# Four-layer sandwich kernel on one core: gathers, sums, first loads, rank products and late statistics take other places in the order written out by hand

## The reference

```
x = x + LN(ssm(LN(x)))       # A: selective state space scan with a short convolution
x = x + LN(moe(LN(x)))       # B: 8 experts, top 2
x = x + LN(attn(LN(x)))      # C: gated attention in groups of 32, with a linear part
x = x + LN(ffn(LN(x)))       # D: silu(x Wg) * (x Wu), then Wd
# moe: out += ((a * sigmoid(b)) @ Wo.T + bo) * comb[e],  a, b = split(x @ W1[e].T + b1[e])
```

## Time and profile before

| | us |
|---|---|
| median of 3 runs | 582.27 (581.85 to 584.56) |
| profiled execution, its own time | 578.57 |
| its span | 576.8 |
| PE busy, DVE busy | 484.9, 455.9 |
| POOL busy, ACT busy | 310.9, 306.6 |

### The profile page before, as it was taken

The page is one execution under the profiler, slowest core; times in us unless marked ns, Lnnn a source line. Parts: engine busy times, 40 slices in busy tenths (PEclk is TensorE's granted clock), DMA queues, the critical chain, the costliest instruction groups (busy, mean ns, idle before and its releaser), DMA issues.

```text
span 576.8 us, 11015 instructions
## 1 busy us (share of the span) xinstructions
PE 484.9 (84%) x3102; PEld 396.1 (69%) x3102; DVE 455.9 (79%) x1742; ACT 306.6 (53%) x655; POOL 310.9 (54%) x349
## 2 busy tenths in 40 slices
PE   7998998899898987678678687888888998889990
PEld 3555787697786866456555465777888897778890
DVE  3885678999898899967574467888888988799974
ACT  3767775667657562244243344565555566445531
POOL 5852553726677667657432657377787232224342
PEclk9999998999999999999798798999999999999996
DMA  7704999900000001335356764321212000000111
GB/s 192 233 2 119 286 285 285 276 6 9 20 25 15 27 11 36 91 105 173 123 166 183 218 197 147 118 56 56 73 50 63 1 2 0 2 1 20 37 38 55
DMA packets 74213, 54.87 MB, mean 95 GB/s; under 512 B 5665, under 2 KB 69665, under 8 KB 74154
## 3 DMA queue, kind: packets, MB, share of 16 engines
q1 hardware_dynamic: 69034, 41.58, 24.6%
q0 software_dynamic: 5120, 12.59, 7.5%
HBM read 19.70 MB, written 34.45 MB: 94 GB/s over the span
## 4 chain that ended last, share of the span: by engine, by line
PE 39%; issue 21%; DVE 18%; POOL 12%; ACT 5%; DMA 1%; SPq 1%; another core or an unknown queue 1%; POOLq 0%; DVEq 0%; ACTq 0%
PE ps L1907 5%; POOL z_rows L557 5%; PE ps L1909 4%; PE ps L1908 4%; POOL tails L705 2%; PE ps L2303 2%; PE ps L2369 2%; POOL work L680 2%; DVE rstats_t L1248 2%; PE ps L2228 2%; PE ps L2371 2%; DVE X L1210 1%; PE ps L2128 1%; PE ps L2394 1%; PE ps L1924 1%
## 5 line engine op out<-in xcount | busy, mean ns | idle before, releaser
L570 POOL DMA_INDIRECT shared_buf<-g_rows,back x64 | 64.1, 1001 | 37.5 <-DVE slot_g L1693 21.4
L557 POOL DMA_INDIRECT z_rows<-Z,dest x64 | 64.3, 1004 | 24.5 <-issue 16.6
L1907 PE MATMUL ps<-w_hi,ZT_hi 128*128 (+1 forms) x110 | 47.8, 435 | 18.3 <-issue 11.9
L823 ACT ACTIVATE Z<-X,shift,rstds 128x128 f32<-128x128 f32 x128 | 53.3, 484 | 11.8 <-DVE shift L1174 8.6
L1009 ACT ACTIVATE half_tanh<-ps 128x256 f32<-128x256 f32 x78 | 29.2, 384 | 53.7 <-PE ps L1909 40.7
L542 POOL TENSOR_TENSOR rstds<-vars_t,mhalf 128x4 f32<-128x4 f32 (+1 forms) x24 | 31.4, 1308 | 47.5 <-DVE vars_t L1197 24.8
L1693 DVE SCALAR_TENSOR_TENSOR slot_g<-half_tanh,ps 128x256 f32<-128x256 f32 x78 | 31.5, 416 | 29.8 <-ACT half_tanh L1009 17.5
L547 POOL TENSOR_TENSOR res_rstd<-rvar,mhalf 128x4 f32<-128x4 f32 x24 | 25.2, 1051 | 38.8 <-DVE rvar L1265 38.8
L1908 PE MATMUL ps<-w_lo,ZT_hi 128*128 (+1 forms) x110 | 41.7, 379 | 0.0
L1909 PE MATMUL ps<-w_hi,ZT_lo 128*128 (+1 forms) x110 | 41.4, 377 | 0.0
L1907 PEld LDWEIGHTS ps<-w_hi,ZT_hi 128*128 128x128 f32 x110 | 21.9, 199 | 27.5 <-issue 26.4
(11 more groups left out here) (359 smaller groups left out, 1568.3 us busy)
## 6 DMA issues: line engine op xcount, KB each, us to landing
z_rows<-zero SPq DMA_DIRECT2D x34, 512.0 KB, 6.6
g_rows<-slot_g SPq DMA_DIRECT2D x38, 256.0 KB
slot_zs<-z_rows SPq DMA_DIRECT2D x78, 64.0 KB
X<-in_x SPq DMA_DIRECT2D x4, 512.0 KB, 6.5
RES<-in_W1T SPq DMA_DIRECT2D x4, 512.0 KB, 5.6
out<-X SPq DMA_DIRECT2D x7, 256.0 KB, 2.3
z_rows<-Z,dest POOLq DMA_INDIRECT x64
shared_buf<-g_rows,back POOLq DMA_INDIRECT x64
```

Source lines behind the costliest of these rows:

```text
L557: pool.indirect_dma_start(z_rows[group(i)], bass.IndirectOffsetOnAxis(ap=dest[:, i, k, c:c + 1], axis=0), Zr[i % 4][:, c], None).then_inc( ...
L570: pool.indirect_dma_start(got[:, c, k], None, g_rows[group(i)], bass.IndirectOffsetOnAxis(ap=back[:, i, k, c:c + 1], axis=0))\
L823: act.activation(dst[:, c], X[:, i, c], ACT.Identity, bias=bias[:, c:c + 1], scale=rstd[:, c:c + 1]).then_inc(z_made, 1)
L1907: pe.matmul(dst, lh, rh, start=start, stop=False)
```

## The change

`gather(t)` waits for tile 2t + 4 of group 1 instead of 2t + 1. The sums and what hangs on them come two tiles later (`MOE_AT`, statistics). Of the fourteen calls of `SCATTER_TILE` the last eleven wait one or two tiles longer. The loads of group 1's first quad stand behind the store of tile 35, those of the next three behind the store of tile 38. On PE the rank computation stands behind the tile's product, and its five identity products are left out in the tile stage. Two powers and, at the end, `lastD(6)` move. The diff, with unchanged lines left out:

```diff
-        SCATTER_TILE = ((4, 2, 0), (4, 3, 2), (5, 0, 5), (5, 1, 7), (5, 2, 9), (5, 3, 11), (6, 0, 13), (6, 1, 15),
-                        (6, 2, 17), (6, 3, 19), (7, 0, 21), (7, 1, 23), (7, 2, 25), (7, 3, 27))
-        LATE_LOADS = {33: 0, 35: 1, 37: 2, 38: 3}
+        SCATTER_TILE = ((4, 2, 0), (4, 3, 2), (5, 0, 5), (5, 1, 9), (5, 2, 11), (5, 3, 13), (6, 0, 15), (6, 1, 17),
+                        (6, 2, 19), (6, 3, 20), (7, 0, 22), (7, 1, 24), (7, 2, 26), (7, 3, 28))
+        LATE_LOADS = {35: (0,), 38: (1, 2, 3)}
...
-        MOE_AT = (8, 10, 12, 14, 16, 18, 20, 22, 24, 26, 28, 30)
+        MOE_AT = (10, 12, 14, 16, 18, 20, 22, 24, 26, 28, 30, 32)
...
                     if g == 0 and j in LATE_LOADS:
-                        load_quad(QUADS.index((1, LATE_LOADS[j])))
+                        for late in LATE_LOADS[j]:
+                            load_quad(QUADS.index((1, late)))
...
-                if (i, c) == (5, 1):
+                if (i, c) == (5, 0):
                     power(1, SEQS - 1)
             for t in range(4 * CH):
-                pool.wait_ge(g_made, GTILES[0] + 2 * t + 2)
+                if t == 12:
+                    power(2, 0)
+                pool.wait_ge(g_made, GTILES[0] + 2 * t + 5)
                 gather(t)
                 if t == 9:
                     res_power(2, 0)
-                if t == 12:
-                    power(2, 0)
...
-                    if g == 1 and j == 30:
+                    if g == 1 and j == 32:
                         z(2, 0)
...
-                    if g == 1 and j in (20, 28):
-                        rbn_stats(2, (j - 20) // 8)
-                    if g == 1 and j in (21, 29):
-                        rbn_aggr(2, (j - 21) // 8)
-                    if g == 1 and j in (24, 33):
-                        x_add(2, (j - 24) // 9)
-                    if g == 1 and j == 25:
+                    if g == 1 and j in (22, 30):
+                        rbn_stats(2, (j - 22) // 8)
+                    if g == 1 and j in (23, 31):
+                        rbn_aggr(2, (j - 23) // 8)
+                    if g == 1 and j in (26, 35):
+                        x_add(2, (j - 26) // 9)
+                    if g == 1 and j == 27:
                         bn_stats(2, 0)
-                    if g == 1 and j == 26:
+                    if g == 1 and j == 28:
                         bn_aggr(2, 0)
-                    if g == 1 and j == 29:
+                    if g == 1 and j == 31:
                         scales(2, 0)
...
-                if half == 0:
-                    lastD(SEQS - 2)
             rbn_aggr(4, i)
+            lastD(SEQS - 2)
...
-                        for k in range(5):
-                            pe.matmul(bank(2)[:, 3 * P:4 * P], ident[:], ident[:], start=True, stop=True)
+                        if step < NT:
+                            for k in range(5):
+                                pe.matmul(bank(2)[:, 3 * P:4 * P], ident[:], ident[:], start=True, stop=True)
...
-                        elif j > 2:
-                            gate(NT + j // 2 - 1, 2)
                     slot_h(GFIRST[g] + j, n, j, experts[j - 4 * q])
+                    if g == 0 and 2 < j and j % 2 == 1 and NT + j // 2 - 1 < GATE_END:
+                        gate(NT + j // 2 - 1, 2)
```

## The result

In six executions of each, the kernel before had a median of 583.17 us (578.9 to 588.24) and the changed kernel 587.12 us (584.44 to 589.28). The ratio is 1.0098, with a 95% interval of 1.0067 to 1.0129: slower by about 1%. The changed kernel was timed twice more among the experiments, at 1.0058 [1.0022, 1.0093] and 1.0177 [1.0105, 1.0249]. The forecast of 579.1 was wrong, and 587.12 lies 1.1 above its range. The nearest of its cases is rival 2, the hole ahead of quad 1, at 585.6. That it comes so near is partly luck: its sum holds +4.3 us for a hole that measured +2.5.

The account below looks back on a forecast made before the run. Waits, not full engines, were taken to bound the tiles. Terms −1.5 + 0.8 + 2.8 − 3.0 − 1.0 − 1.25 = −3.15 us, carried to the median shown of 582.27, gave 579.1 us, range 573.5 to 586.0.

Parts of the forecast that it names:

- rival 2: Group 1's start: quad 1's loads wait for tile 38's gate, PE idles, clock falls again; +3.4 us, 585.6; chance 0.20.
- Late signals go by half: Tiles 8 to 11 of group 1: later gathers remove half of two 3.2 us ACT waits for PE; −3.0 us.
- the powers: POOL in group 1: its 2.66 us wait behind gather 9 for DVE's statistics nearly goes; −1.0 us.
- Rival 1: Group 1's gathers: POOL soon issues without a pause again, late signals stay; +0.35 us, 582.6; chance 0.24.
- Quads 1 to 3 behind the last store: Start of group 1: quad 1's loads wait for tile 38's gate and land after PE needs them; +2.8 us.
- Rank part with the scatters: Group 0: products ahead of ranks, no identity products, gain 2.8 us, limited by later scatters; −1.5 us together.
- the scatters bound the group from behind: End of group 0: six calls left instead of five, scatters end at 298.0, first loads start at 299 to 302.
- Quad 0 behind the store of tile 35: Between the groups: group 1's first loads wait for tile 35's gate and start 1.3 us later; taken as +0.8 us.
- Tail: Kernel's end: last statistics and power start earlier, one full DVE wait for POOL's addition stays; −1.25 us.

Follow-up runs that it names:

- c_best: Kernel before with the rank, gather and tail parts, without late loads and scatters: 573.60 us, 0.9890; again 577.96 us, 0.9949.
- a_loads: Changed kernel with group 1's first loads back behind the stores of tiles 33, 35, 37 and 38: 579.76 us, 0.9977 to the kernel before.
- c_nogather: Kernel before with the rank and tail parts alone, on the faster chip: 556.76 us, 0.9985.
- c_power: c_best with only the power of sequence 7 moved ahead of call (5, 1), on the faster chip: 559.45 us, 1.0035 to the kernel before.

## Why the prediction was wrong, step by step

1. *Late signals go by half (−3.0), and the powers (−1.0)*: this step failed, and it is the largest part of the miss that a run prices. The part alone measured −0.14%, 0.8 us, with zero in its interval, which ends at 0.9953; −4.0 us would be 0.993. Undone in the changed kernel, nothing came back. The trace shows why. I counted on the gaps between pairs of gathers. But the first gather moved with the first tiles from 311.73 to 320.44, tiles then ran ahead of POOL at about 1 us each, and ten gathers still stood nearly in one row. One late signal of 3.87 us stood at its end, where there had been two of 3.2. The wait of POOL for the statistics, counted as gone, is still 2.44 of 2.66 us. Rival 1, by which POOL soon issues without a pause again, was right in its mechanism.

2. *Quads 1 to 3 behind the last store (+2.8)*: right in mechanism, and in size for the hole. The hole from gate to gate is 2.5 us longer in the profile after, and 2.2 to 4.2 longer in the eight other profiles with quad 1 late. The point from which rival 2 was to decide, a PE idle time over 3 us and the lower clock behind it, was not met in the first profile: the idle time is 1.38 us, since the products ahead of it ran at the lower clock already and used up the rest. In the second profile of the changed kernel it was met (3.11 us, and 0.63 us for a product behind it), in the third it was 2.42. But filling the hole so that the clock held brought nothing back.

3. *Rank part with the scatters (−1.5)*: one sum for two things of opposite sign. The ranks alone give −0.40%, 2.3 us, but nothing in the changed kernel, where the transpose at tile 21 came 0.35 us earlier and not 2.1: I left out that the picks can come late by themselves. The scatter tiles cost: +0.3% alone (unclear), 0.9% between c_best and a_loads, about 0.8% on the faster chip. I had the last one end at 298.0, from two instructions more in the last burst; it ended at 301.25, since the pause before ended 1.9 us later and another tile was waited for. The step that failed is "the scatters bound the group from behind". On the slower chips no profile has a scatter in the chain ahead of the first load. What stands there in its place is a scatter row without pauses in group 0 and a late signal at its end; that this is how the scatters cost is argued from the profiles and not shown by a run of its own. The end of POOL's queue counts only on the faster chip (in three of its four profiles), and there I should have looked at all of its waits: POOL has 24 such instructions to its end, and a call that waits earlier moves all behind it.

4. *Quad 0 behind the store of tile 35 (+0.8)*: the first transpose came 2.95 us later. But gates up to tile 35 were late by 2.87 already, so this edit's own part is small, and putting quad 0 back brought nothing. Part of those 2.87 us can't be laid on the change: tile 5 was 2.0 us late (257.05 to 259.01), and so it was in the kernel with later gathers alone (259.24), which is the same up to there.

5. *Tail (−1.25)*: right, 1.45 us. The operation on four columns takes 1.25 us beside POOL's addition of 1.26 and ends with it; an operation of the same size takes 0.15 just ahead of it. The wait only moved to another of DVE's instructions. The Trainium skill states this in "SBUF — State Buffer", "SBUF: two separate sides": of a VectorE operation with two SBUF inputs and a GpSimd operation, the one that starts first has the shared ports for its whole length. The trace agrees: POOL's started at 573.95, DVE's at 573.97.

With 0.8 instead of 4.0 in step 1, my sum gives 582.3, within 0.5% of before. The other 4.8 us to 587.12 are the scatters, what the loads cost beyond their term, and the ranks' gain that is not there. The three measurements of the whole lie between +0.6 and +1.8%, so no division in microseconds holds for all of them. But it is known where the surplus sits: ranks, gathers and tail together measured 0.9890 and 0.9949, about their sum of 0.992, and the two costly parts cost more in company than alone (scatters 0.9 against 0.3%, loads 0.8 to 1.0 against 0.5%). Why they do is open; that parts cost more where PE waits less otherwise is argued, not shown. Also open is why the changed kernel has a lower clock between 223 and 290, ahead of the moved loads: 0.77, 0.85 and 0.87 in its three profiles, against 0.95 before. With the ranks and identity products back it was 0.92; but the ranks alone had 0.85 there and were faster, and the gathers alone, with the identity products, had 0.87.

## What to carry to other kernels

A wait that is put in front of a load is paid nearly in full when the consumer is only a few tiles behind (2.5 of 2.8 us here); read the distance from the load's issue to its use, and move only what is needed late (here quads 2 and 3 at most, and not quad 1). Delaying the start of a queue of long instructions doesn't thin it out if its producers run faster than the queue: count how many are ready when it starts. And price a table of waits over the whole queue, each entry by the wait that it can add, and edits of opposite sign in separate terms, so that an experiment can answer each. What a part is worth alone need not be what it is worth in company: the ranks' 0.4% was gone in the changed kernel.

## What was not expected of the hardware

- The chips differ. The kernel before took 581.2 to 583.2 us in five groups of runs and 557.5 in one, 4.3% less. On that chip the long waits of ACT for PE in the tile stage are nearly all gone, as the group of tanh of the whole page shows (busy, mean ns, idle before and its first releaser), for the ranks alone on a slower chip and then for c_nogather, which is the same kernel but for the tail (the kernel before has no profile from the faster chip):

```profile
L1009 ACT ACTIVATE half_tanh<-ps 128x256 f32<-128x256 f32 x78 | 28.8, 384 | 53.3 <-PE ps L1909 37.5
```
```profile
L1009 ACT ACTIVATE half_tanh<-ps 128x256 f32<-128x256 f32 x78 | 29.3, 382 | 37.3 <-PE ps L1908 36.2
```

  So the late signals belong to the chip as much as to the order of the work. Ranks and tail had little to gain there (0.9985), and with the later gathers and the power (1, 7) added nothing was left (c_power, 1.0035).
- Late signals stand near the end of unbroken rows of indirect transfers issued by POOL, in every profile of the slower chips: ACT's idle time is 5.17 us in the changed kernel and up to 6.06 (the scatters alone, at 322.64). Such a row is not enough by itself: on the faster chip POOL issued the 22 scatters of c_power without a wait, and ACT had no idle time over 2.3 us beside them. What delays the signals no run here tells.
- Time and granted clock go together over one kernel's executions. In 35 of the kernel before, time and mean clock have a correlation of −0.77 and a slope of −3.9 us per 0.01 of clock; without the six slowest it is −0.59 and −2.3. The changed kernel beside before had 0.9492 against 0.9547, which at these slopes is 1.3 to 2.1 of the 2.3 us between their medians; which of the two is the cause this doesn't tell.
- The twelve loads issued in a row took 0.62 us each (7.44 / 12), the four at 304.45 took 0.47.
